# Cross-attention over 8 sequences: chunks of turned probabilities handed over singly, and one transpose moved ahead

## The chip, the cores and the metric

The kernel runs on one core of one Trainium2 chip. The metric is the time of one launch in microseconds (us) on the device. PE is TensorE, DVE is VectorE, ACT is ScalarE, POOL is GpSimd, and SP is SyncE, whose queue issues nearly all the DMAs.

## The reference

For each of 8 sequences of 1024 rows and 640 features, with 20 heads of 32 features, and an encoder context of 64 tokens, of which the last 8 are image tokens and 56 are text:

```python
q = split_heads(x @ w_q)
out_text = softmax(q @ k_text.T / sqrt(32)) @ v_text
out_ip   = softmax(q @ k_ip.T / sqrt(32) + box_mask) @ v_ip
out = (merge(out_text) + merge(out_ip)) @ w_out + b_out + x
```

`k_text`, `v_text`, `k_ip` and `v_ip` are projections of the context, and the mask depends on whether a row's grid position lies in one of four boxes.

## The kernel before

A setup (about the first 106 us) projects keys and values. After it the work goes in 16 groups `g` (`NG` is 16), each of 512 rows (`GQ`), two groups for each sequence (`GPB` is 2). A group has five chunks `m` of four heads each and ten pairs `p` of heads; chunk `m` holds pairs `2m` and `2m + 1`. Every product of the projections is made of three float32r products of high and low parts, `hi*hi + hi*lo + lo*hi`, so the tiles `xT`, `pT`, `oT` each have a `_hi` part, rounded by ACT, and a `_lo` part, the difference, made by DVE or POOL.

The groups are pipelined. While PE does the value products of group `g` (`pv_pair`, L1207 and L1208), it also makes the scores of group `n = g + 1` (L199), the output projection of groups `g - 1` and `g` (`out_step`) and the query projection of group `x = g + 2` (`q_steps`); the last two are matmuls of L101 to L103. Each engine runs an order written out by hand; a group has five slots on each engine, numbered nought to four, and slot `s` of PE begins with `pv_pair(g, 2s)` and `pv_pair(g, 2s + 1)`, followed by the scores of chunk `s` of `n`.

A chunk of probabilities passes these steps:

1. ACT copies the scores out of PSUM (`copy_scores`, L206); POOL adds the mask (`add_mask`, L242); DVE takes the maxima (`maxima`, L219); POOL subtracts them (`sub_max`, L248); ACT exponentiates (L211).
2. DVE sums and takes the reciprocal (`sums`, L225 and L227); POOL multiplies by it (`normalise`, L255) and raises `prob_done`.
3. DVE transposes 32x32 blocks into one of three stage buffers (`turn`, L236). `turn` waits for `prob_done` of its own chunk, and for the write to DRAM of the chunk three before it.
4. SP writes the stage to DRAM (`write_out`, L469) and, once that write has landed, reads it back rearranged in four DMAs (`read_back`, L474).
5. ACT makes `pT_hi` (L746) of each pair when the chunk has landed; DVE (even pairs, L981) or POOL (odd pairs, L599) makes `pT_lo`; PE multiplies.

The output of a pair goes by `move_pv` on ACT (L751) and `add_pv` on DVE (L991), then `oT_hi` on ACT (L755) and `oT_lo` on POOL (L595). `output` on DVE (L997) finishes a block of the result in `res`, SP stores it (L516) and reloads `res` (L490) once the store has landed.

In slot two of group `g` DVE has, in order, `add_pv(g, 4)`, `add_pv(g, 5)`, `pT_part(g, 6)`, `sums(n, 1)`, `maxima(n, 2)`, `turn(n, 0)`, `turn(n, 1)`, with `output(g - 1, 4)` after these in group 14 only, and then slot three begins: `add_pv(g, 6)`, `add_pv(g, 7)`, `pT_part(g, 8)`, `maxima(n, 3)`, `sums(n, 2)`. POOL's order there is `sub_max(n, 1)`, `normalise(n, 0)`, `add_mask(n, 2)`, `oT_part(g, 2)`, `normalise(n, 1)`, `sub_max(n, 2)`, `add_mask(n, 3)`, `pT_part(g, 9)`, `oT_part(g, 3)`, `sub_max(n, 3)`, `normalise(n, 2)`, `add_mask(n, 4)`, `normalise(n, 3)`, `pT_part(n, 1)`, `oT_part(g, 4)`. In slot four DVE has `add_pv(g, 8)`, `add_pv(g, 9)`, then for odd `g` the low parts of the next sequence's values (L425), then `sums(n, 3)`, `turn(n, 2)`, `maxima(n, 4)`, `pT_part(n, 0)`, `pT_part(n, 2)`, `turn(n, 3)`.

Group 14 is the last that prepares another one, and it has no queries of a next group to project. Its SP order has `store(13, 4)` and `load_res(14, 4)` between chunks 1 and 2 of group 15, and `store(13, 3)` with `load_res(14, 3)` ahead of chunk 0.

Of the kernel before, what the change touches and what calls it, by code (L numbers as in the profile page):

```python
# [29 lines left out]
def attention_kernel(nc, xT_dram, textT, ipT, bbox, w_q, w_k, w_v, w_k_ip, w_v_ip, w_out, b_out, grid_x, grid_y, outT):  # L30
# [30 lines left out]
    with whole:  # L61
# [54 lines left out]
        def x_lo_part(dve, g, k):  # L116
            dve.wait_ge(xT_hi_done, KD * g + k + 1)
            nc.vector.tensor_tensor(x_tile(xT_lo, k), x_of(g)[:, k, :], x_tile(xT_hi, k).bitcast(F32), ALU.subtract).then_inc(xT_lo_done, 1)
# [35 lines left out]
        def load_k(sp, b):  # L154
            sp.dma_start(k_raw[:].rearrange("p m k -> p (m k)"), k_scratch[:, b, :]).then_inc(k_raw_loaded, 16)
# [23 lines left out]
        def in_dram(eng, n):  # L179
            wait(eng, written[n % S_RING], 16 * (n // S_RING + 1))  # L180
# [3 lines left out]
        def chunk(m):  # L184
            return prob[:, m * CHUNK:(m + 1) * CHUNK].rearrange("p (r k) -> p r k", k=KEYS)
# [36 lines left out]
        def sums(dve, g, m):  # L222
            dve.wait_ge(exp_done, KD * g + m + 1)
            for n, (k0, k1) in enumerate(SPANS):
                nc.vector.tensor_reduce(total[:, m, n, :], chunk(m)[:, :, k0:k1], AX.X, ALU.add).then_inc(sum_done, 1)  # L225
            dve.wait_ge(sum_done, 2 * (KD * g + m + 1))
            nc.vector.reciprocal(inv[:, m, :, :], total[:, m, :, :]).then_inc(inv_done, 1)  # L227

        def turn(dve, g, m):

            n = KD * g + m
            dve.wait_ge(prob_done, n + 1)
            in_dram(dve, n - S_RING)
            src = prob[:, m * CHUNK:(m + 1) * CHUNK].rearrange("p (t h c i) -> p t h c i", t=GT, h=2, i=QUAD)
            dst = stage[:, n % S_RING].rearrange("p c h (t i) -> p t h c i", i=QUAD)
            nc.vector.transpose(dst, src).then_inc(turned, 1)  # L236
# [190 lines left out]
        with nc.Block() as block:  # L427

            @block.sync
            def _(sp):  # L430
# [34 lines left out]
                def write_out(g, m):  # L465
                    n = KD * g + m
                    sp.wait_ge(turned, n + 1)
                    wait(sp, pT_landed[m], 16 * QUADS * g)
                    sp.dma_start(p_scratch[m], stage[:, n % S_RING].rearrange("p c h t -> p (c h t)")).then_inc(written[n % S_RING], 16)  # L469

                def read_back(g, m):
                    in_dram(sp, KD * g + m)
                    for c in range(QUADS):
                        sp.dma_start(prob[c * QUAD:(c + 1) * QUAD, m * CHUNK:(m + 1) * CHUNK].rearrange("i (q f) -> i q f", q=QUADS),  # L474
                                     p_scratch[m].rearrange("(q i) (c f) -> c i q f", q=QUADS, c=QUADS)[c]).then_inc(pT_landed[m], 16)

                def hand_over(g, ms):
                    for m in ms:
                        write_out(g, m)
                    for m in ms:  # L480
                        read_back(g, m)

                def load_x(g):
                    sp.wait_ge(xT_lo_done, KD * (g - 1))
                    for k in range(KD):
                        sp.dma_start(x_of(g)[:, k, :], x_half[g % 2, g // 2][:, k, :]).then_inc(x_loaded[g % 2], 16)

                def load_res(g, m):
                    wait(sp, stored[m], 16 * g)
                    sp.dma_start(res[:, m, :], x_half[g % 2, g // 2][:, m, :]).then_inc(res_loaded[m], 16)  # L490
# [17 lines left out]
                def load_v(b):  # L508
                    sp.wait_ge(v_built, 2 * b)
                    for h in range(2):  # L510
                        sp.dma_start(v_raw[h * KEYS:h * KEYS + NTEXT, :], v_scratch.rearrange("(b k) d -> b k d", b=B)[b]).then_inc(v_raw_loaded, 16)
                        sp.dma_start(v_raw[h * KEYS + NTEXT:(h + 1) * KEYS, :], v_ip_scratch.rearrange("(b k) d -> b k d", b=B)[b]).then_inc(v_raw_loaded, 16)

                def store(g, m):
                    sp.wait_ge(out_done, outs_before(g, m) + 1)
                    sp.dma_start(out_half[g % 2, g // 2, m], res[:, m, :]).then_inc(stored[m], 16)  # L516
# [8 lines left out]
                for g in range(NG):  # L525
                    b = g // GPB
                    if g + 3 < NG:
                        load_x(g + 3)
                    if g > 0:
                        for m in range(3) if g == NG - 2 else OUT_ORDER:  # L530
                            store(g - 1, m)
                    hand_over(g, (4,))
                    for m in range(3) if g == NG - 2 else OUT_ORDER:
                        load_res(g, m)
                    if g == NG - 2:
                        store(g - 1, 3)
                        load_res(g, 3)
                    if g % GPB == 0 and b < B - 1:
                        sp.wait_ge(k_built, HPT * (b + 1))
                        load_k(sp, b + 1)  # L540
                        load_v(b + 1)
                    if g + 1 < NG:
                        hand_over(g + 1, (0, 1))
                        if g == NG - 2:
                            store(g - 1, 4)
                            load_res(g, 4)
                        hand_over(g + 1, (2, 3))
                for m in OUT_ORDER:
                    store(NG - 1, m)
                for m in range(KD):  # L550
# [316 lines left out]
            def _(dve):  # L867
# [138 lines left out]
                for g in range(NG):  # L1006
                    n, x = g + 1, g + 2
                    more, more_x = n < NG, x < NG

                    if more_x and g > 0:  # L1010
                        x_lo_part(dve, x, 0)
                    add_pv(g, 0)
                    add_pv(g, 1)
                    if g == 0:
                        maxima(dve, n, 0)
                        x_lo_part(dve, x, 0)
                    if more_x:
                        x_lo_part(dve, x, 1)
                        x_lo_part(dve, x, 2)
                    if 0 < g != NG - 2:  # L1020
                        output(g - 1, 3)
                    if more_x:
                        x_lo_part(dve, x, 3)
                    if g > 0:
                        sums(dve, g, 4)
                        if g != NG - 2:
                            output(g - 1, 4)
                        output(g - 1, 0)
                    if more and g > 0:
                        maxima(dve, n, 0)  # L1030
                    if g > 0:
                        output(g - 1, 1)
                        output(g - 1, 2)
                    if more_x:
                        x_lo_part(dve, x, 4)

                    add_pv(g, 2)
                    pT_part(g, 4)
                    add_pv(g, 3)
                    turn(dve, g, 4)  # L1040
                    if more:
                        maxima(dve, n, 1)
                        sums(dve, n, 0)
                    if g == NG - 2:
                        output(g - 1, 3)

                    add_pv(g, 4)
                    add_pv(g, 5)
                    pT_part(g, 6)
                    if more:  # L1050
                        sums(dve, n, 1)
                        maxima(dve, n, 2)
                        turn(dve, n, 0)
                        turn(dve, n, 1)
                    if g == NG - 2:
                        output(g - 1, 4)

                    add_pv(g, 6)
                    add_pv(g, 7)
                    pT_part(g, 8)  # L1060
                    if more:
                        maxima(dve, n, 3)
                        sums(dve, n, 2)

                    add_pv(g, 8)
                    add_pv(g, 9)
                    if more and n % GPB == 0:
                        v_lo_part(dve, n // GPB)
                    if more:
                        sums(dve, n, 3)  # L1070
                        turn(dve, n, 2)
                        maxima(dve, n, 4)
                        pT_part(n, 0)
                        pT_part(n, 2)
                        turn(dve, n, 3)
# [243 lines left out]
```

## Time and profile before

| | |
|---|---|
| time, median of 3 runs | 815.95 us (814.95 to 816.05) |
| the profiled execution | 814.83 us, span 813.0 us |
| granted TensorE clock, mean | 0.989 of full speed |
| PE busy | 794.7 us (98%) |
| DVE busy | 677.0 us (83%) |
| POOL busy | 629.1 us (77%) |
| ACT busy | 540.7 us (67%) |
| time of packets on SP's queue | 64.7% of 16 DMA engines |

Times inside the trace run from the start of the span. A row's start and duration are of one instruction or of several alike that follow each other ("x2"), and the bracket gives the idle time of the engine ahead of it and what ended that. A `tensor_reduce` or `normalise` of a chunk is two instructions, for the text keys and for the image keys, so one `sums` or one `sub_max` is a row of "x2". The group in which something happens can be told by PE: group 0 begins at 106.6, group 14 at 736.5 and group 15 at 774.65 us.

### The profile page before, as it was taken

The page shows a single profiled execution, that of the slowest core. Times are in us where ns is not written, and L with a number is a line of the kernel's source. Part 1 is how long each engine was busy: PE and PEld are TensorE (multiplying, and loading weights), DVE is VectorE, ACT ScalarE, POOL GpSimd, SP SyncE. Part 2 cuts the span into 40 slices and gives each one's busy share as a digit, 9 for nine tenths or more (in the row PEclk, how much of TensorE's full clock was granted, in tenths as well). Part 3 has the DMA queues.
Part 4 walks back from the last instruction along what each step waited for, and adds up shares of the span by engine and source line. Part 5 has one row for each costly group of instructions (what it writes and reads, how often), then busy time and mean ns, then how long its engine had stood idle before and what let it go on. Part 6 is the DMA issues. An engine that isn't in the chain of part 4 may idle for free.

```text
span 813.0 us, 12922 instructions
## 1 busy us (share of the span) xinstructions
PE 794.7 (98%) x4381; PEld 648.5 (80%) x4381; DVE 677.0 (83%) x983; ACT 540.7 (67%) x928; POOL 629.1 (77%) x576
## 2 busy tenths in 40 slices
PE   9999989999999999999999999999999999999887
PEld 8889867888788878888788888878887888787666
DVE  6938779889878897889878898889878888889973
ACT  7767367677586667666685767666775767676642
POOL 0049749797987888797979888797979888789972
PEclk9999989999999999999999999999999999999899
DMA  9943596765766577765766477665766476565664
GB/s 315 384 136 114 160 287 217 206 232 145 243 209 221 186 233 220 233 206 138 261 193 217 164 234 244 207 220 156 270 186 221 148 245 210 169 195 168 208 202 160
DMA packets 104177, 169.99 MB, mean 209 GB/s; under 512 B 13104, under 2 KB 56112, under 8 KB 103984
## 3 DMA queue, kind: packets, MB, share of 16 engines
q1 hardware_dynamic: 103968, 167.86, 64.7%
q10 hardware_dynamic: 144, 1.31, 0.4%
q8 instruction: 35, 0.57, 0.3%
q14 instruction: 30, 0.25, 0.1%
HBM read 103.26 MB, written 65.54 MB: 208 GB/s over the span
## 4 chain that ended last, share of the span: by engine, by line
PE 85%; POOL 6%; ACT 3%; DVE 2%; issue 1%; DMA 1%; SPq 1%; DVEq 0%; ACTq 0%
PE bank L101 22%; PE bank L102 21%; PE bank L103 21%; PE bank L199 9%; PE bank L1207 4%; PE bank L1208 4%; POOL prob L248 2%; POOL prob L255 1%; PE bank L1094 1%; PE bank L1102 1%; POOL wo_lo L558 1%; PE bank L1106 1%; POOL pT_lo L599 1%; ACT prob L206 1%; DVE stage L236 1%
## 5 line engine op out<-in xcount | busy, mean ns | idle before, releaser
L751 ACT ACTIVATE pv_part<-bank 64x512 f32<-64x512 f32 x160 | 94.7, 592 | 168.2 <-PE bank L1208 165.9
L248 POOL TENSOR_TENSOR prob<-prob,top 128x896 f32<-128x896 f32 (+1 forms) x160 | 183.0, 1164 | 13.3 <-DVE top L219 13.1
L255 POOL TENSOR_TENSOR prob<-prob,inv 128x896 f32<-128x896 f32 (+1 forms) x160 | 172.7, 1101 | 9.6 <-DVE inv L227 8.4
L991 DVE TENSOR_TENSOR o_raw<-bank,pv_part 64x512 f32<-64x512 f32 x160 | 110.1, 688 | 59.2 <-ACT pv_part L751 55.8
L101 PE MATMUL bank<-oT_hi,wo_hi 128*128 128x512 f32 x375 | 154.0, 411 | 2.4 <-POOL oT_lo L595 2.4
L101 PE MATMUL bank<-xT_hi,wq_hi 128*128 128x512 f32 x400 | 156.2, 390 | 0.0
L102 PE MATMUL bank<-xT_lo,wq_hi 128*128 128x512 f32 x400 | 155.9, 390 | 0.0
L103 PE MATMUL bank<-xT_hi,wq_lo 128*128 128x512 f32 x400 | 155.9, 390 | 0.0
L599 POOL TENSOR_TENSOR pT_lo<-prob,pT_hi 128x512 fp32r<-128x512 f32 x80 | 116.0, 1451 | 41.9 <-ACT pT_hi L746 41.8
L103 PE MATMUL bank<-oT_hi,wo_lo 128*128 128x512 f32 x375 | 146.7, 391 | 0.0
L102 PE MATMUL bank<-oT_lo,wo_hi 128*128 128x512 f32 x375 | 146.6, 391 | 0.0
L595 POOL TENSOR_TENSOR oT_lo<-o_raw,oT_hi 128x512 fp32r<-128x512 f32 x75 | 103.5, 1381 | 49.4 <-ACT oT_hi L755 47.9
L225 DVE TENSOR_REDUCE total<-prob 128x16 f32<-128x896 f32 (+1 forms) x160 | 101.8, 678 | 3.6 <-ACT prob L211 3.4
L219 DVE TENSOR_REDUCE top<-prob 128x16 f32<-128x896 f32 (+1 forms) x160 | 99.7, 664 | 4.0 <-ACT prob L206 2.6
L199 PEld LDWEIGHTS bank<-k_diag,qT 64*128 64x128 f32 x1280 | 79.1, 191 | 27.6 <-issue 22.4
L236 DVE STREAM_TRANSPOSE stage<-prob 128x1024 f32<-128x1024 f32 x80 | 96.7, 1223 | 0.9
L746 ACT ACTIVATE pT_hi<-prob 128x512 fp32r<-128x512 f32 x160 | 93.4, 624 | 4.4 <-DMA prob<-p_scratch 3.5
L199 PE MATMUL bank<-k_diag,qT 64*128 64x128 f32 x1280 | 94.1, 288 | 0.0
L206 ACT ACTIVATE prob<-bank 128x512 f32<-128x512 f32 x160 | 85.6, 592 | 12.2 <-PE bank L199 12.2
L211 ACT ACTIVATE prob<-prob 128x1024 f32<-128x1024 f32 x80 | 84.5, 1056 | 8.2 <-POOL prob L248 7.5
L101 PEld LDWEIGHTS bank<-oT_hi,wo_hi 128*128 128x128 f32 x375 | 70.3, 187 | 24.3 <-POOL oT_lo L595 3.5
L101 PEld LDWEIGHTS bank<-xT_hi,wq_hi 128*128 128x128 f32 x400 | 75.3, 188 | 15.8 <-issue 0.2
(111 smaller groups left out, 1276.1 us busy)
## 6 DMA issues: line engine op xcount, KB each, us to landing
p_scratch<-stage SPq DMA_DIRECT2D x80, 512.0 KB, 3.0
prob<-p_scratch SPq DMA_DIRECT2D x320, 128.0 KB, 3.1
res<-in_xT SPq DMA_DIRECT2D x80, 256.0 KB, 4.9
outT<-res SPq DMA_DIRECT2D x80, 256.0 KB, 3.9
xin<-in_xT SPq DMA_DIRECT2D x75, 256.0 KB, 4.7
w_raw<-in_L_xattn_w_k SPq DMA_DIRECT2D x8, 320.0 KB, 5.4
w_raw<-in_L_xattn_w_k_ip SPq DMA_DIRECT2D x8, 320.0 KB, 5.7
w_raw<-in_L_xattn_w_v_ip SPq DMA_DIRECT2D x8, 320.0 KB, 4.7
```

What stands on the lines that cost most here:

```text
L101: nc.tensor.matmul(dst, a_hi, b_hi, start=first, stop=False)
L102: nc.tensor.matmul(dst, a_hi, b_lo, start=False, stop=False)
L103: return nc.tensor.matmul(dst, a_lo, b_hi, start=False, stop=last)
L199: ins = nc.tensor.matmul(s_bank(g, 2 * m + r)[:, t * PW:(t + 1) * PW], qT[rows, m, q_cols], k_diag[rows, m, :], start=True, stop=True)
L219: ins = nc.vector.tensor_reduce(top[:, m, n, :], chunk(m)[:, :, k0:k1], AX.X, ALU.max)
L225: nc.vector.tensor_reduce(total[:, m, n, :], chunk(m)[:, :, k0:k1], AX.X, ALU.add).then_inc(sum_done, 1)
L236: nc.vector.transpose(dst, src).then_inc(turned, 1)
L248: ins = nc.gpsimd.tensor_tensor(s, s, top[:, m, n, :].unsqueeze(2).broadcast_to([P, ROWS, k1 - k0]), ALU.subtract)
L255: ins = nc.gpsimd.tensor_tensor(s, s, inv[:, m, n, :].unsqueeze(2).broadcast_to([P, ROWS, k1 - k0]), ALU.mult)
L595: nc.gpsimd.tensor_tensor(oT_at(oT_lo, g, m), o_raw[:, (KD * g + m) % 2, :], oT_at(oT_hi, g, m).bitcast(F32), ALU.subtract).then_inc(oT_lo ...
L599: nc.gpsimd.tensor_tensor(pT_part_at(pT_lo, g, p), pT(p), pT_part_at(pT_hi, g, p).bitcast(F32), ALU.subtract).then_inc(pT_lo_pool, 1)
L991: nc.vector.tensor_tensor(by_quadrant(raw), a, c, ALU.add).then_inc(pv_added, 1)
```

## The change

SP handles the chunks 0 to 3 of the next group one by one: it writes a chunk, waits for it to land, and issues its four reads, before it turns to the next chunk. Before, it wrote two and then read two. The first two hand-overs of group 0, ahead of the loop, stay couples. On DVE `turn(n, 0)` goes ahead of `sums(n, 1)` and `maxima(n, 2)`; `turn(n, 1)` stays where it was.

```diff
                     if g + 1 < NG:
-                        hand_over(g + 1, (0, 1))
+                        hand_over(g + 1, (0,))
+                        hand_over(g + 1, (1,))
                         if g == NG - 2:
                             store(g - 1, 4)
                             load_res(g, 4)
-                        hand_over(g + 1, (2, 3))
+                        hand_over(g + 1, (2,))
+                        hand_over(g + 1, (3,))
...
                     if more:
+                        turn(dve, n, 0)
                         sums(dve, n, 1)
                         maxima(dve, n, 2)
-                        turn(dve, n, 0)
                         turn(dve, n, 1)
```

## Rows read from the trace of the kernel before

**Rows 1.** Busy time by stretch: span, PE, PEld, DVE, ACT, POOL, clock, DMA share, GB/s
```profile
305.30:350.40 45.10, 45.10 (x254) 36.34 (x252) 37.53 (x56) 31.52 (x55) 37.78 (x36) 1.00 0.69 216
```

**Rows 2.** Timeline of PE: its waits in group 0 and in group 14
```profile
125.31 0.50 PE L101 MATMUL bank<-oT_hi,wo_hi 128*128 128x512 f32 x1 [0.64 <-POOL oT_lo L595]
...
764.64 0.77 PE L1207 MATMUL bank<-pT_hi,v_parts 128*128 128x512 f32 x1 [2.68 <-DVE pT_lo L981]
...
774.65 0.76 PE L1207 MATMUL bank<-pT_hi,v_parts 128*128 128x512 f32 x1 [2.66 <-DVE pT_lo L981]
```

**Rows 3.** Timeline of DVE, group 14, slots two and three
```profile
755.66 1.27 DVE L225 TENSOR_REDUCE total<-prob 128x16 f32<-128x896 f32 x2
756.96 0.35 DVE L227 RECIPROCAL inv<-total 128x32 f32<-128x32 f32 x1
...
758.36 2.60 DVE L236 STREAM_TRANSPOSE stage<-prob 128x1024 f32<-128x1024 f32 x2
...
763.09 1.41 DVE L981 TENSOR_TENSOR pT_lo<-prob,pT_hi 128x512 fp32r<-128x512 f32 x1
```

**Rows 4.** Timeline of POOL, group 14, slots two and three
```profile
753.50 2.50 POOL L255 TENSOR_TENSOR prob<-prob,inv 128x896 f32<-128x896 f32 x2
...
757.62 2.05 POOL L255 TENSOR_TENSOR prob<-prob,inv 128x896 f32<-128x896 f32 x2
759.64 2.06 POOL L248 TENSOR_TENSOR prob<-prob,top 128x896 f32<-128x896 f32 x2
...
762.68 1.27 POOL L599 TENSOR_TENSOR pT_lo<-prob,pT_hi 128x512 fp32r<-128x512 f32 x1 [0.56 <-ACT pT_hi L746]
```

**Rows 5.** Timeline of DVE, group 0, slots two and three
```profile
132.10 2.60 DVE L236 STREAM_TRANSPOSE stage<-prob 128x1024 f32<-128x1024 f32 x2
...
136.17 1.71 DVE L981 TENSOR_TENSOR pT_lo<-prob,pT_hi 128x512 fp32r<-128x512 f32 x1
```

**Rows 6.** Timeline of POOL, group 0, slots two and three
```profile
127.23 2.51 POOL L255 TENSOR_TENSOR prob<-prob,inv 128x896 f32<-128x896 f32 x2
...
136.03 1.30 POOL L599 TENSOR_TENSOR pT_lo<-prob,pT_hi 128x512 fp32r<-128x512 f32 x1 [0.17 <-ACT pT_hi L746]
```

**Rows 7.** Timeline of PE, group 0, the first matmul of slot four
```profile
138.55 0.39 PE L1207 MATMUL bank<-pT_hi,v_parts 128*128 128x512 f32 x1
```

**Rows 8.** Timeline of DVE, group 9, slots two, three and four
```profile
534.07 0.70 DVE L981 TENSOR_TENSOR pT_lo<-prob,pT_hi 128x512 fp32r<-128x512 f32 x1
...
541.73 0.69 DVE L981 TENSOR_TENSOR pT_lo<-prob,pT_hi 128x512 fp32r<-128x512 f32 x1
...
553.50 1.75 DVE L981 TENSOR_TENSOR pT_lo<-prob,pT_hi 128x512 fp32r<-128x512 f32 x1
```

**Rows 9.** Timeline of POOL, group 9, slot three
```profile
542.23 1.35 POOL L599 TENSOR_TENSOR pT_lo<-prob,pT_hi 128x512 fp32r<-128x512 f32 x1 [1.31 <-ACT pT_hi L746]
```

**Rows 10.** Timeline of PE, group 9 slot four and group 10 slot nought
```profile
544.75 0.39 PE L1207 MATMUL bank<-pT_hi,v_parts 128*128 128x512 f32 x1
...
555.82 0.39 PE L1207 MATMUL bank<-pT_hi,v_parts 128*128 128x512 f32 x1
```

**Rows 11.** Timeline of SP's queue, group 14: start and time of the issues
```profile
761.70 0.85 SPq L469 DMA_DIRECT2D p_scratch<-stage  x2
765.62 3.65 SPq L474 DMA_DIRECT2D prob<-p_scratch  x8
...
773.22 4.46 SPq L469 DMA_DIRECT2D p_scratch<-stage  x2
```

**Rows 12.** DMA issues of the page: size of each, median us to landing
```profile
p_scratch<-stage SPq DMA_DIRECT2D x80, 512.0 KB, 3.0
prob<-p_scratch SPq DMA_DIRECT2D x320, 128.0 KB, 3.1
```

**Rows 13.** Timeline of ACT: the waits for a landing in group 14, and group 15
```profile
744.01 1.15 ACT L746 ACTIVATE pT_hi<-prob 128x512 fp32r<-128x512 f32 x2 [2.15 <-DMA prob<-p_scratch]
...
788.85 1.15 ACT L746 ACTIVATE pT_hi<-prob 128x512 fp32r<-128x512 f32 x2
```

## The prediction

> **What bounds the kernel.** I read the busy times by stretch first. In a stretch of one period of the steady part, 45.1 us, PE is busy for all of it at the full granted clock (2.4 GHz), while DVE has 37.5 us of work and POOL 37.8 us [rows 1]. So PE alone sets the pace there; DVE, POOL and SP have cover, and nothing that the change does to them can make that part shorter. It can make it longer, where DVE or POOL come later than PE's next matmul needs them.
>
> Next I looked for PE's own waits. After the setup there are few. In group 0 there is one of 0.64 us [rows 2]. In group 14 there are two long ones, 2.68 us ahead of `pv_pair(14, 8)` and 2.66 us ahead of `pv_pair(15, 0)`, both ended by a `pT_lo` of DVE [rows 2]. Group 14 projects no queries, so PE has less work there than the two engines that feed it. The chain of waits runs there through POOL and then DVE, and touches just the slot that is edited: `turn(15, 1)` ends, then come `output(13, 4)`, two `add_pv` and `pT_part(14, 8)`, for which PE waits [rows 3].
>
> Last I read the order of DVE, POOL and SP around slot two, in group 14, in group 0, and in group 9 as one of the steady groups.
>
> **The change on DVE.** It adds no instruction; it moves a transpose of 1.25 us ahead of `sums(n, 1)` and `maxima(n, 2)`. Two things follow. `turn(n, 0)` must find `prob_done` of chunk 0 raised. And `sums(n, 1)` comes later, so `normalise(n, 1)` on POOL starts later, while between the sums and `turn(n, 1)` there is now one pair of maxima as cover in place of maxima and a transpose. Before, the second transpose found its chunk ready almost at once: two of them took 2.60 us for 2.50 us of work [rows 3].
>
> *Group 14.* `normalise(15, 0)` ends at 753.50 + 2.50 = 756.00 [rows 4]. DVE would have been free at 755.66 [rows 3], so it waits 0.4 us; the transpose runs from 756.04 and frees DVE at about 757.25. From the start of the sums to the end of the reciprocal it is 756.96 + 0.35 - 755.66 = 1.65 us [rows 3], so the reciprocal is there at 758.9. POOL, which before began `normalise(15, 1)` at 757.62 [rows 4], now begins at 758.95 and ends, with 2.05 us, at 761.0. DVE's maxima end at about 760.0, so DVE stands for 1 us, and `turn(15, 1)` ends at 762.3 in place of 760.96 [rows 3]: 1.35 us late. From there to the start of `pT_part(14, 8)` it was 763.09 - 760.96 = 2.13 us, so that now starts at 764.4. It took 1.41 us [rows 3] against 0.69 us in group 9 [rows 8], because POOL's `pT_part(14, 9)` was on its way; DVE ended 0.55 us after POOL's 762.68 + 1.27 = 763.95. POOL's own `pT_part(14, 9)` follows `sub_max(15, 2)` and a mask. That was 2.48 us from 759.64, less a wait of 0.56 us that falls away, but 0.46 us for the mask remains; it now starts at 761.0 + 2.06 + 0.4 = about 763.4 and ends at 764.65 [rows 4]. DVE then ends at 765.2 in place of 764.50, so the price is **0.7 us**. Its bounds are 0.6 us (if DVE gets in ahead of POOL, 764.4 + 0.7 = 765.1) and 1.35 us (the whole lateness). I take 0.7, since POOL's place shows which engine is ahead. What comes next moves with it: `maxima(15, 3)`, POOL's subtraction, the exponential, `sums(15, 3)`, `turn(15, 2)` and `pT_part(15, 0)` are the chain to the second wait of PE [rows 2], and from there to slot one of group 15 PE works without a wait. Nothing gives the 0.7 us back.
>
> *Group 0.* `normalise(1, 0)` ends at 127.23 + 2.51 = 129.74 [rows 6]. By the same steps: transpose to 130.95, reciprocal at 132.6, `normalise(1, 1)` to 134.75, `turn(1, 1)` to 136.05 in place of 132.10 + 2.60 = 134.70 [rows 5]. `pT_part(0, 8)` started 1.47 us after that end [rows 5] and now starts at 137.5. POOL, 1.3 us late as well, has `pT_part(0, 9)` from 137.15 to 138.45 (it took 1.30 us [rows 6]), so DVE ends 0.55 us behind that, at 139.0. PE starts 0.14 us after such an end (764.50 to 764.64 in group 14), at 139.15; it was due at 138.55 [rows 7]. The price is **0.6 us**, with nought as the lower bound: were DVE ahead of POOL, it would end at 138.2 and hide. A short wait like the one of 0.64 us costs itself: the first matmul after it took 0.50 us, those after long waits 0.77 us [rows 2].
>
> *The steady groups.* In group 9 `normalise` of chunk 0 is long done when DVE is through with `pT_part(9, 6)` at 534.77 [rows 8]. The transpose, the sums and the reciprocal end at 534.7 + 1.2 + 1.65 = 537.5; POOL ends `normalise(10, 1)` at 539.65, and `turn(10, 1)` ends at 540.9, 1.2 us later than before. Part of it goes into a wait of DVE for `pv_part` that was there. `pT_part(9, 8)` arrives at 542.4 in place of 541.73 [rows 8], and this time POOL's `pT_part(9, 9)`, which starts at 542.23 [rows 9], is ahead. With 1.29 us for POOL and 0.55 us behind it DVE ends at 544.1 in place of 542.4. PE needs it at 544.75 [rows 10], so with 0.14 us it is hidden with 0.5 us left. In odd groups DVE has the values' low parts in slot four, and there the rest of the lateness, 0.35 us, gets through to `pT_part(10, 0)`. That ended at 553.50 + 1.75 = 555.25 [rows 8] and will end at 555.6; PE needs it at 555.82 [rows 10]. With 0.14 us that is hidden by less than 0.1 us. I take **nothing** for the 14 groups between; from the other side it is 0.3 us in each of the 7 odd ones, 2.1 us.
>
> The Trainium skill (SBUF — State Buffer, "SBUF: two separate sides") calls the port pair that DVE and GpSimd share an exclusive lock: whichever starts first has it for the whole instruction. By it the three prices hang on who arrives first, and by its rule alone, with DVE first, the sum would be 0.6 us less, from group 0. The trace agrees with the lock: 1.41 and 1.71 us against 0.69 us for one and the same instruction.
>
> **The change on SP.** It adds no DMA, but each couple becomes two round trips. Couple 2 and 3: `turn(n, 3)` comes 5 us after `turn(n, 2)`, so write and reads of chunk 2 fit in between, chunk 2 lands about 3 us earlier, and chunk 3 as before. Couple 0 and 1: chunk 0 is read earlier, and the write of chunk 1 now stands behind the landing and the four reads of chunk 0, so chunk 1 lands later: about 3 us, a landing of 3.0 us [rows 12], where SP comes late. In the steady groups ACT asks for chunk 1 more than 10 us after its transpose: hidden. In group 14 SP gets to chunk 0 at 761.70 [rows 11], behind a reload of `res`, so the earlier transpose brings nothing there.
>
> Then it adds up. The reads of the couple ended at 765.62 + 3.65 = 769.27 [rows 11]. Now: chunk 0 read by 767.4, chunk 1 written then, landed 3.0 us on and read by 772.3. Store and reload took SP 773.22 - 769.27 = 3.95 us before the write of chunk 2 [rows 11], now at 776.2; landed 779.2, read by 781.1, chunk 3 written, landed 784.1, read by 785.9, and in place 3.1 us later [rows 12], at **789.0**. ACT takes chunk 3 at 788.85 + 0.6 + 0.6 [rows 13], that is at 790.1 with the 0.7 and 0.6 us of PE. It is hidden with 1 us left. If each landing takes 3.92 us, as 761.70 to 765.62 did [rows 11], chunk 3 comes at 791.8 and costs 1.7 us.
>
> The Trainium skill (DMA: Bandwidth & Descriptors, "Anatomy of one DMA") puts a DMA at about 2.0 us fixed plus its bytes at 436 GB/s. For 512 KB that is an estimate of 3.2 us, between the two of this trace; by it four landings add 0.8 us to 789.0 and the chunk is still in time. The rule speaks against the change all the same: a second fixed cost is paid for each couple.
>
> **The sum.** 0.7 + 0.6 = 1.3 us on the profiled execution's 814.83 us. That execution lies 1.1 us under the median of the runs, so against the median of 815.95 us it is **817.2 us**, 0.16% more. What a measurement of this kernel can tell from no change is 0.2%, 1.6 us, so this counts as the same.
>
> **The rivals.**
>
> *A. Late chunk 3 in group 15.* SP's four round trips in a row run past 790.1. For it: there is only 1 us left, and landings of 3.9 us occur [rows 11]. Against it: the median is 3.0 us [rows 12]. It gives 817.2 + 0 to 1.7, say 818.3 us.
>
> *B. The steady cover gives way.* PE waits for `pT_part(n, 0)` in the odd groups. For it: a margin under 0.1 us by my own steps. Against it: PE has no wait there now, and a later PE gives the others more time. 7 x 0.3 us give 817.2 + 2.1 = 819.3 us.
>
> *C. Nothing shows.* DVE arrives ahead of POOL in group 0, and some of group 14's lateness is absorbed: 0 to 0.6 us, 816.2 us.
>
> *D. Faster, by the earlier chunk 2 of group 14.* ACT stood for 2.15 us for its landing at 744.01 [rows 13]. With the reads of chunk 2 issued about 3 us earlier this wait goes. It decides only if `pT_part(14, 4)` or `(14, 5)` hold the chain there. Against it: in the chain of waits it is POOL that works there without a pause, and its row shows no wait for `pT_hi` before the one of 0.56 us [rows 4]. If all 2.15 us came through, the time would be 815.95 - 2.15 = 813.8 us.
>
> **Chances.** The forecast (0.7 and 0.6 us, each within its bounds) 0.47, A 0.15, B 0.15, C 0.14, D 0.09. The forecast's own range is 816.5 to 817.9 us, and some 0.1 of its 0.47 lies beyond 1.6 us. Slower: 0.15 + 0.15 + 0.1 = 0.40, less 0.01 of A that stays under. Faster: D. The rest, 0.52, is the same. The range of 8 in 10 takes in A, most of B and C: 815.6 to 819.6 us.
>
> **What would show it.** In the profile after: `turn(15, 0)` begins at 756.0 plus what was lost before, DVE idles about 1 us ahead of `turn(15, 1)`, released by POOL's L255; PE's wait ahead of `pv_pair(14, 8)` grows from 2.68 to about 3.4 us; in group 0 a wait of PE of 0.6 us appears ahead of L1207; none in groups 1 to 13; ACT's wait of 2.15 us at 744 is gone; SP has writes of x1 in place of x2. I am wrong if PE waits in the steady groups, if `pT_part(15, 6)` waits for a landing, or if the order of DVE and POOL at the shared work is the other one.

## The result, and the profile after

The changed kernel takes 819.88 us (median of 6 runs, 817.39 to 823.73), the kernel before 815.08 us (6 runs, 813.39 to 816.05). The ratio is 1.0066, with a 95% interval of 1.0041 to 1.0091: slower by about 5 us. (A ratio here is an estimate from all the runs of both kernels, and not the quotient of the two medians, which is 1.0059; what is said of single parts of the time comes from profiled executions.) I had 817.2 us with a range up to 819.6, and "the same" as the likeliest. So the size was missed, and the median lies outside the range. Both numbers are medians of runs; against 815.08 my sum of 1.3 us would have been 816.4.

The profiled execution took 817.39 us, span 815.6, which is the fastest of the six. Its span is 2.6 us longer than that of the kernel before; a second profiled execution of the same kernel, shown further down, took 819.05 us.

Of PE's waits in the changed kernel these four bear on the account, from its timeline. The first answers to a matmul that waited for nothing before [rows 7], the last two to [rows 2]:

```profile
138.44 0.47 PE L1209 MATMUL bank<-pT_hi,v_parts 128*128 128x512 f32 x1 [0.34 <-DVE pT_lo L983]
...
603.49 1.16 PE L199 MATMUL bank<-k_diag,qT 64*128 64x128 f32 x16 [1.16 <-ACT qT L142]
...
767.20 0.77 PE L1209 MATMUL bank<-pT_hi,v_parts 128*128 128x512 f32 x1 [3.36 <-DVE pT_lo L983]
...
777.20 0.77 PE L1209 MATMUL bank<-pT_hi,v_parts 128*128 128x512 f32 x1 [2.66 <-DVE pT_lo L983]
```

The first and the third are the two prices that I had put into the sum. In group 14 the wait is 3.36 - 2.68 = 0.68 us longer (forecast 0.7); counted from the scores of slot nought of that group, the matmul starts after 767.20 - 739.03 = 28.17 us in place of 764.64 - 737.35 = 27.29, so the group loses 0.88 us, and 0.2 us of it fall ahead of the place that I had looked at, 0.1 of them at a matmul that waits for `res` (0.44 in place of 0.33 us). In group 0 the row shows 0.34 us of idle time, but matmuls overlap in the trace, so the loss is read from starts: from the scores of slot three to those of slot four it took PE 131.27 to 139.52, 8.25 us, in place of 131.88 to 139.55, 7.67 us. That is 0.58 us (forecast 0.6). The second I had not: at the turn from group 10 to group 11 PE waits 1.16 us for the last query tile before it can make scores.

DVE in group 14, the answer to [rows 3]. The transpose of chunk 0 waits 0.30 us for `normalise(15, 0)`, that of chunk 1 waits 1.03 us for `normalise(15, 1)`:

```profile
757.92 1.25 DVE L236 STREAM_TRANSPOSE stage<-prob 128x1024 f32<-128x1024 f32 x1 [0.30 <-POOL prob L255]
759.09 1.24 DVE L225 TENSOR_REDUCE total<-prob 128x16 f32<-128x896 f32 x2
760.36 0.35 DVE L227 RECIPROCAL inv<-total 128x32 f32<-128x32 f32 x1
...
762.88 1.25 DVE L236 STREAM_TRANSPOSE stage<-prob 128x1024 f32<-128x1024 f32 x1 [1.03 <-POOL prob L255]
...
766.26 0.79 DVE L983 TENSOR_TENSOR pT_lo<-prob,pT_hi 128x512 fp32r<-128x512 f32 x1
```

DVE in group 9, the answer to [rows 8]. `pT_part(9, 8)` takes 1.72 us in place of 0.69, because POOL's `pT_part(9, 9)` now starts ahead of it (at 542.49, and 542.61 for DVE):

```profile
542.61 1.72 DVE L983 TENSOR_TENSOR pT_lo<-prob,pT_hi 128x512 fp32r<-128x512 f32 x1
```

What is new is in SP's queue. Group 10 in the changed kernel, start and time of each issue (L469 writes a chunk, L474 reads it back, L490 reloads `res`):

```profile
578.20 2.56 SPq L490 DMA_DIRECT2D res<-in_xT  x5
...
582.84 0.34 SPq L469 DMA_DIRECT2D p_scratch<-stage  x1
589.70 1.74 SPq L474 DMA_DIRECT2D prob<-p_scratch  x4
591.54 0.38 SPq L469 DMA_DIRECT2D p_scratch<-stage  x1
597.38 1.73 SPq L474 DMA_DIRECT2D prob<-p_scratch  x4
```

The reads of a chunk are issued when its write has landed. So the write of chunk 0 took 6.86 us and that of chunk 1 another 5.84 us. The first is no exception: in groups 0 to 13 the write of chunk 0 takes 5.3 to 7.0 us. The second is: the write of chunk 1 takes 3.2 to 4.2 us in the others, and over 5 only in groups 10 and 11; no run shows what held it there. The last read of chunk 1 is issued at 599.1. And ACT, whose timeline at that place is

```profile
601.32 0.63 ACT L748 ACTIVATE pT_hi<-prob 128x512 fp32r<-128x512 f32 x1 [2.88 <-DMA prob<-p_scratch]
601.85 0.58 ACT L142 ACTIVATE qT<-bank 128x512 f32<-128x512 f32 x1
602.33 0.62 ACT L748 ACTIVATE pT_hi<-prob 128x512 fp32r<-128x512 f32 x1
602.85 0.59 ACT L142 ACTIVATE qT<-bank 128x512 f32<-128x512 f32 x1
```

stands 2.88 us for chunk 1, in `pT_part(11, 2)`. Behind it in ACT's order are `move_q(12, 3)`, `pT_part(11, 3)` and, as the first of group 11, `move_q(12, 4)` at 602.85. PE's scores of group 12 need that one; they start at 603.49. The product that chunk 1 is for comes a slot later and was not held up.

In group 9, an odd one, the same part of SP's queue before, and then after:

```profile
538.66 1.46 SPq L469 DMA_DIRECT2D p_scratch<-stage  x2
542.39 3.64 SPq L474 DMA_DIRECT2D prob<-p_scratch  x8
```

```profile
533.72 2.33 SPq L490 DMA_DIRECT2D res<-in_xT  x5
536.20 0.33 SPq L469 DMA_DIRECT2D p_scratch<-stage  x1
542.76 1.75 SPq L474 DMA_DIRECT2D prob<-p_scratch  x4
```

The totals by waiting engine say the same. Waits of ACT for the landing of a chunk were 3.5 us in 3 places before; after, in sum, times and longest:

```profile
ACT pT_hi L748 <- DMA prob<-p_scratch: 17.8, 12, 3.1
...
SPq L474 <- DMA p_scratch<-stage: 274.2, 78, 6.6
```

The chain of waits ends, in place of PE and POOL work, with SP's four round trips for the chunks of group 15. This is its part from the write of chunk 2 to POOL's `pT_part(15, 7)`; the columns are start, duration, and what the chain goes through:

```profile
778.07 4.08 DMA p_scratch<-stage
...
784.01 3.27 DMA p_scratch<-stage
...
788.59 2.78 DMA prob<-p_scratch
791.37 0.02 issue
791.39 0.02 ACT pT_hi L748
...
792.62 1.30 POOL pT_lo L601
```

Chunk 3 lands at 791.37, and ACT takes it at 791.39. That the chain runs there does not mean that it costs much: PE's wait behind it, ahead of `out_step(15, m, 1)`, is 1.37 us, and was 1.35 us before.

### The profile page after: what moved, and what is told of

Same layout as the page of the kernel before. It is cut to its first block, busy times and chain, and to the rows that moved or that the text cites. A ratio compares the mean times of both kernels' runs of the same rounds, so it can differ in the third digit from the quotient of the medians.

```text
span 815.6 us, 12922 instructions
## 1 busy us (share of the span) xinstructions
PE 795.1 (97%) x4381; PEld 647.5 (79%) x4381; DVE 689.7 (85%) x983; ACT 542.0 (66%) x928; POOL 634.4 (78%) x576
## 4 chain that ended last, share of the span: by engine, by line
PE 79%; POOL 8%; DVE 4%; DMA 3%; ACT 3%; SPq 2%; issue 1%; DVEq 0%; ACTq 0%
PE bank L101 21%; PE bank L102 19%; PE bank L103 19%; PE bank L199 9%; PE bank L1209 4%; PE bank L1210 4%; POOL prob L248 3%; POOL prob L255 2%; DMA p_scratch<-stage 2%; SPq L474 1%; PE bank L1096 1%; DVE stage L236 1%; PE bank L1104 1%; POOL pT_lo L601 1%; POOL wo_lo L560 1%
## 5 line engine op out<-in xcount | busy, mean ns | idle before, releaser
L597 POOL TENSOR_TENSOR oT_lo<-o_raw,oT_hi 128x512 fp32r<-128x512 f32 x75 | 107.3, 1430 | 47.5 <-ACT oT_hi L757 47.5
L748 ACT ACTIVATE pT_hi<-prob 128x512 fp32r<-128x512 f32 x160 | 94.6, 625 | 18.8 <-DMA prob<-p_scratch 17.8
L983 DVE TENSOR_TENSOR pT_lo<-prob,pT_hi 128x512 fp32r<-128x512 f32 x80 | 92.6, 1165 | 12.5 <-ACT pT_hi L748 11.2
```

The source lines that it names most:

```text
L597: nc.gpsimd.tensor_tensor(oT_at(oT_lo, g, m), o_raw[:, (KD * g + m) % 2, :], oT_at(oT_hi, g, m).bitcast(F32), ALU.subtract).then_inc(oT_lo ...
```

## The experiments

All ratios are to the kernel before, run on the same chip in the same job.

**The two parts apart.** First the moved transpose alone, with couples on SP (the edit is against the changed kernel):

```diff
-                        hand_over(g + 1, (0,))
-                        hand_over(g + 1, (1,))
+                        hand_over(g + 1, (0, 1))
...
-                        hand_over(g + 1, (2,))
-                        hand_over(g + 1, (3,))
+                        hand_over(g + 1, (2, 3))
```

> The moved transpose alone; SP hands over in couples as before. Theory 1 (the loss is chunk 1 that lands late by SP's serial round trips, and ACT stands for it with the queries behind): here chunk 1 is written with chunk 0 and lands in time, so only the two places at the ends remain, 0.34 us in group 0 and 0.68 us ahead of pv_pair(14, 8): ratio 1.001 to 1.002, no wait of PE in groups 1 to 13. Theory 2 (the loss is DVE and POOL, 1.2 us later in each slot two): nearly the whole loss is here, ratio 1.005 or more, with PE waits for pT_lo or oT_lo in the steady groups.

Measured: 816.04 us, ratio 1.0020 (1.0012 to 1.0029). Its waits of PE are those of the sum, the one of 0.34 us in group 0 and

```profile
765.89 0.77 PE L1207 MATMUL bank<-pT_hi,v_parts 128*128 128x512 f32 x1 [3.44 <-DVE pT_lo L981]
```

and none for `qT`. Theory 2 falls. This part alone costs about what I had forecast for the whole. By its profile it is 0.6 us in group 0, 0.5 us in the steady groups (the table further down) and 0.9 us from the scores of group 14 to the end.

Then SP's single hand-over alone, with DVE's order as before (against the changed kernel):

```diff
-                        turn(dve, n, 0)
                         sums(dve, n, 1)
                         maxima(dve, n, 2)
+                        turn(dve, n, 0)
                         turn(dve, n, 1)
```

> SP hands over singly, DVE's order as before. Theory 1: most of the loss is here, ratio 1.003 to 1.006; ACT waits for landings 8 times or more, some over 2.5 us, and where they are over 2.5 us PE waits for qT ahead of the scores of the next slot nought. Theory 2: ratio 0.999 to 1.001.

Measured: 818.37 us (12 runs, 815.52 to 821.23), ratio 1.0045 (1.0030 to 1.0060). ACT waits for landings in 11 places, up to 4.15 us, and PE for `qT` in two; one of them, and the place in group 15 where chunk 3 is late, from the timelines of PE and ACT:

```profile
332.07 1.16 PE L199 MATMUL bank<-k_diag,qT 64*128 64x128 f32 x16 [0.48 <-ACT qT L142]
...
796.16 0.50 PE L101 MATMUL bank<-oT_hi,wo_hi 128*128 128x512 f32 x1 [1.74 <-POOL oT_lo L597]
...
792.36 1.16 ACT L748 ACTIVATE pT_hi<-prob 128x512 fp32r<-128x512 f32 x2 [0.41 <-DMA prob<-p_scratch]
```

That last wait of PE was 1.35 us in the kernel before. The two parts together give 1.0020 x 1.0045 = 1.0065, beside 1.0066 for the change. The intervals are 0.2 to 0.5% wide, so that the two agree so closely is luck.

**Which couple.** Only chunks 2 and 3 singly:

```diff
                         hand_over(g + 1, (0, 1))
...
-                        hand_over(g + 1, (2, 3))
+                        hand_over(g + 1, (2,))
+                        hand_over(g + 1, (3,))
```

> Only chunks 2 and 3 singly, chunks 0 and 1 as a couple, DVE's order as before. Theory 1: chunk 1 lands in time, chunk 2 sooner: ratio 0.998 to 1.001, no wait of PE in the steady groups, ACT's wait of 2.15 us at 744 moves to chunk 3. Theory 2: the same. If it is over 1.003, the loss comes from chunks 2 and 3 and both fall.

Measured: 814.53 us, ratio 0.9997 (0.9989 to 1.0006). The transposes of these two begin about 5 us apart on DVE (551.23 and 556.87 in group 9 before), so splitting them alone costs nothing and gains nothing. The loss needs chunks 0 and 1 split.

**What stands behind the late chunk.** The changed kernel, with ACT's order so that no query move follows the landing:

```diff
                         pT_part(n, 0)
                         pT_part(n, 1)
-                        pT_part(n, 2)
                     if more_x:
                         move_q(act, x, 3)
-                    if more:
-                        pT_part(n, 3)
...
                         if more:
                             move_q(act, n, 4)
+                        pT_part(g, 2)
+                        pT_part(g, 3)
```

and DVE with `turn(n, 3)` ahead of `pT_part(n, 2)`.

> The changed kernel, but ACT makes pT_hi(n, 2) and (n, 3) behind both of the query moves that follow them (move_q(x, 3) and the next group's move_q(n, 4)), and DVE turns chunk 3 ahead of pT_part(n, 2). Chunk 1 lands as late as in the changed kernel, but nothing of the queries stands behind it. Theory 1: the steady loss goes, PE has no wait for qT, ratio 1.001 to 1.003 (what is left is that of the transpose alone). Theory 2: the loss stays, 1.005 or more.

Measured: 817.86 us (817.73 to 818.99), ratio 1.0042 (1.0029 to 1.0054). It lies between the two theories' numbers. PE has no wait for `qT`, and ACT's waits for landings fall from 17.8 us in 12 places to

```profile
ACT pT_hi L748 <- DMA prob<-p_scratch: 3.9, 3, 2.6
```

with the steady ones gone. The write of chunk 0 is as slow as in the changed kernel (5.5 to 6.9 us in groups 0 to 13), so the wait of PE for `qT` comes by way of ACT's order: that is the mechanism of theory 1. By time alone this run does not show it, for its interval overlaps that of the change. What is left is more than the transpose, and the profile says where: the steady part is 1.25 us longer than before, 0.51 of which are the transpose's, with steps of up to 0.23 us at the end of odd groups, and from the scores of group 14 on it is 0.5 us longer than with the transpose alone. Chunk 3 does not arrive late here. So this order has a price of its own, about 1.2 us.

**Where the single hand-over costs.** Chunks 0 and 1 singly in groups 0 to 13 only, then all four singly in group 14 only, both with DVE's order as before:

```diff
-                        hand_over(g + 1, (0, 1))
+                        for ms in ((0,), (1,)) if g < NG - 2 else ((0, 1),):
+                            hand_over(g + 1, ms)
```

```diff
-                        hand_over(g + 1, (0, 1))
+                        for ms in ((0, 1),) if g < NG - 2 else ((0,), (1,)):
+                            hand_over(g + 1, ms)
...
-                        hand_over(g + 1, (2, 3))
+                        for ms in ((2, 3),) if g < NG - 2 else ((2,), (3,)):
+                            hand_over(g + 1, ms)
```

> Chunks 0 and 1 singly in groups 0 to 13 alone, a couple in group 14; chunks 2 and 3 a couple everywhere; DVE's order as before. Theory A (the loss of the single hand-over sits in the steady groups: chunk 1 late, ACT, queries): ratio 1.002 to 1.004, waits of PE for qT in the profile of some. Theory B (it sits in group 15, where four round trips of SP in a row end at chunk 3): ratio 0.999 to 1.001.

> All four chunks singly in group 14 alone, couples elsewhere; DVE's order as before. Theory A: ratio 0.999 to 1.001. Theory B: 1.002 to 1.004, and ACT waits for the landing of chunk 3 at about 790 with a wait of PE ahead of out_step(15, m, 1) longer than 1.35 us. Both can hold in part: then this ratio and that of the steady one multiply to 1.0045, the ratio of all hand-overs single.

Measured: 816.57 us, ratio 1.0025 (1.0016 to 1.0035), and 816.12 us, ratio 1.0015 (1.0005 to 1.0026). Both theories hold in part; 1.0025 x 1.0015 = 1.0040, beside 1.0045 for all. The profiled execution of the first was its fastest run (815.26 us), and it shows no wait of PE for `qT` and no loss in the steady part; ACT waited for landings in 14 places, the longest 2.2 us. So its 1.0025 is not seen in its own profile, and that it is the wait for `qT` is taken from the profiles of the other kernels. In the second, ACT waits for chunk 3, and PE behind it 1.92 us in place of 1.35:

```profile
789.28 1.15 ACT L748 ACTIVATE pT_hi<-prob 128x512 fp32r<-128x512 f32 x2 [0.60 <-DMA prob<-p_scratch]
...
793.06 0.50 PE L101 MATMUL bank<-oT_hi,wo_hi 128*128 128x512 f32 x1 [1.92 <-POOL oT_lo L597]
```

That wait accounts for 0.57 us. From the scores of group 14 to the end this execution took 77.38 us, the kernel before 75.65. Most of the other 1.2 us comes of TensorE's clock: behind a wait of 5.49 us ahead of `pv_pair(15, 0)` it was 0.86 up to this wait, against 0.92 before. The eased kernel further down, which has couples there, has the like, 0.85. So of the 1.0015 the late chunk is shown for about half.

**Why the write of chunk 0 is slow.** The changed kernel, with the reloads of `res` behind the hand-over of chunk 1:

```diff
-                    for m in range(3) if g == NG - 2 else OUT_ORDER:
+                    for m in range(3) if g == NG - 2 else () if 0 < g < NG - 2 else OUT_ORDER:
                         load_res(g, m)
...
                         hand_over(g + 1, (1,))
+                        for m in OUT_ORDER if 0 < g < NG - 2 else ():
+                            load_res(g, m)
```

> The changed kernel with the five reloads of res in groups 1 to 13 issued behind the hand-over of chunk 1 in place of ahead of chunk 0, so that the write of chunk 0 does not share the queue with them. If these loads are what keeps the write of chunk 0 at 6 to 7 us, it lands in 3 to 4 us, chunk 1 about 3 us sooner, and ACT's waits in the steady groups go; ratio 1.002 to 1.005 in place of 1.0066. If the write is slow for another reason: ratio as changed, 1.006 to 1.007.

Measured: 817.17 us, ratio 1.0032 (1.0021 to 1.0043). SP in group 9:

```profile
535.53 0.34 SPq L469 DMA_DIRECT2D p_scratch<-stage  x1
538.17 1.73 SPq L474 DMA_DIRECT2D prob<-p_scratch  x4
540.49 0.34 SPq L469 DMA_DIRECT2D p_scratch<-stage  x1
543.27 1.73 SPq L474 DMA_DIRECT2D prob<-p_scratch  x4
545.05 2.33 SPq L490 DMA_DIRECT2D res<-in_xT  x5
```

The write of chunk 0 lands in 2.64 us; in the changed kernel the same one, issued at 536.20, took 6.56 us. In all of groups 1 to 13 it now takes 2.6 to 3.7 us, also in the even ones, where the loads of keys and values still stand ahead of it; in group 0, where the reloads stay in front, it takes 5.97. The waits for landings are gone from groups 1 to 13, and what is left is near the transpose (1.0020) times the end (1.0015). So the loads of 1.25 MB just ahead of it are what holds the write.

**All of it eased.** The single hand-over with both causes removed: `res` late in groups 1 to 13, couples in group 14, DVE's order as before.

```diff
-                    for m in range(3) if g == NG - 2 else OUT_ORDER:
+                    for m in range(3) if g == NG - 2 else () if 0 < g < NG - 2 else OUT_ORDER:
                         load_res(g, m)
...
-                        hand_over(g + 1, (0, 1))
+                        for ms in ((0,), (1,)) if g < NG - 2 else ((0, 1),):
+                            hand_over(g + 1, ms)
+                        for m in OUT_ORDER if 0 < g < NG - 2 else ():
+                            load_res(g, m)
...
-                        hand_over(g + 1, (2, 3))
+                        for ms in ((2,), (3,)) if g < NG - 2 else ((2, 3),):
+                            hand_over(g + 1, ms)
```

> All chunks singly in groups 0 to 13, in groups 1 to 13 with the reloads of res behind chunk 1; couples in group 14; DVE's order as before. If the loss of the single hand-over is made of nothing but the late chunk 1 in the steady groups and the four round trips at the end: ratio 0.999 to 1.001. If a single hand-over has another cost: 1.002 or more.

Measured: 815.70 us against 815.24, ratio 1.0006 (0.9997 to 1.0014). The single hand-over has no third cost that this can tell from nothing. The delay has gone with the loads: in group 9 the write of chunk 0 lands in 2.64 us, and that of chunk 2, now behind them, takes 6.57 us, where no engine but SP waits for it:

```profile
548.18 2.33 SPq L490 DMA_DIRECT2D res<-in_xT  x5
551.22 0.33 SPq L469 DMA_DIRECT2D p_scratch<-stage  x1
557.79 1.75 SPq L474 DMA_DIRECT2D prob<-p_scratch  x4
```

**A second profile of the changed kernel.**

> The changed kernel once more, for a second profile. If its spread (817.4 to 823.7 us) comes from how late chunks land, other groups than group 10 have the wait of PE for qT, and ACT's waits for landings are other ones; the wait of 0.34 us in group 0 and that of 3.4 us ahead of pv_pair(14, 8) are the same.

Measured: 819.05 us. The waits of 0.34 us in group 0 and 3.33 us in group 14 are there again. PE's wait for `qT`, in sum, times and longest, and one of its places:

```profile
PE bank L199 <- ACT qT L142: 2.7, 4, 0.9
...
331.55 1.16 PE L199 MATMUL bank<-k_diag,qT 64*128 64x128 f32 x16 [0.66 <-ACT qT L142]
```

It has four of them, each at the end of an even group, at other groups than the first profile, which had its only one at the turn to group 11 (the end of group 10). The table takes from the timelines of PE the time between the scores of slot nought of group 1 and of group 14:

| kernel | from | to | us |
|---|---|---|---|
| before | 150.62 | 737.35 | 586.73 |
| changed, profile of the 817.39 us | 150.59 | 739.03 | 588.44 |
| changed, profile of the 819.05 us | 149.77 | 740.39 | 590.62 |
| transpose alone | 150.37 | 737.61 | 587.24 |
| single hand-over alone | 150.99 | 739.51 | 588.52 |
| chunks 0 and 1 singly, groups 0 to 13 | 150.94 | 737.70 | 586.76 |
| changed, ACT's order eased | 150.83 | 738.81 | 587.98 |
| changed, `res` late | 149.91 | 737.15 | 587.24 |
| eased | 149.39 | 736.12 | 586.73 |

Beyond the 0.51 us of the transpose the changed kernel loses 1.20 us there in one profile and 3.38 us in the other, of which its waits for `qT` are 1.16 and 2.7 us.

**A version that beats both.** The profile says that DVE's order binds the end of group 14. Two moves there, in group 14 alone, first with chunks 2 and 3 singly, then with all couples:

```diff
-                    if g == NG - 2:
-                        output(g - 1, 4)
...
+                    if g == NG - 2:
+                        output(g - 1, 4)
                     if more:
                         sums(dve, n, 3)
+                        if g == NG - 2:
+                            pT_part(n, 0)
                         turn(dve, n, 2)
                         maxima(dve, n, 4)
-                        pT_part(n, 0)
+                        if g < NG - 2:
+                            pT_part(n, 0)
```

> Chunks 2 and 3 singly with couple 0 and 1, and in group 14 alone DVE makes pT_part(15, 0) ahead of turn(15, 2) and maxima(15, 4), and output(13, 4) only behind add_pv(14, 9). If the end of group 14 is bound by DVE's order, as the two waits of PE say, pv_pair(14, 8) starts some 1.4 us sooner and pv_pair(15, 0) 2 to 3 us sooner, and the end by 1.2 to 1.6 us (pv_pair(15, 1) waits for POOL): ratio 0.998. If POOL alone binds it: 0.9995 to 1.

> The kernel before with the two moves of DVE in group 14 alone (pT_part(15, 0) ahead of turn(15, 2) and maxima(15, 4); output(13, 4) behind add_pv(14, 9)), all hand-overs in couples. If the gain of the run before belongs to DVE's order alone: ratio 0.998 to 0.999. If it needed the single hand-over of chunks 2 and 3: 0.9995 to 1.

Measured: 813.80 us, ratio 0.9986 (0.9977 to 0.9994), and 814.26 us against 815.24, ratio 0.9989 (0.9980 to 0.9998). Both are faster than before, by about 1 us, and the gain is that of DVE's order. PE in the second:

```profile
763.00 0.47 PE L1210 MATMUL bank<-pT_hi,v_parts 128*128 128x512 f32 x1 [1.36 <-DVE pT_lo L981]
...
772.50 0.76 PE L1210 MATMUL bank<-pT_hi,v_parts 128*128 128x512 f32 x1 [4.28 <-DVE pT_lo L981]
774.01 0.77 PE L1210 MATMUL bank<-pT_hi,v_parts 128*128 128x512 f32 x1 [0.31 <-POOL pT_lo L599]
```

From the start of group 14's scores, `pv_pair(15, 0)` begins after 772.50 - 737.06 = 35.4 us in place of 774.65 - 737.35 = 37.3. That is 1.9 us sooner, where 2 to 3 were expected; `pv_pair(14, 8)`, at 763.00, is 1.35 us sooner, as expected.

## Why the prediction was right or wrong

*PE sets the pace of the steady part, and nothing there can be gained.* Right: 586.73 to 586.76 us in the seven kernels that keep DVE's order there and show no wait for `qT`, the kernel before among them.

*Group 14, 0.7 us.* Right, by its steps, for the wait: 0.68 us, with waits of DVE of 0.30 and 1.03 us where I had 0.4 and 1. `pT_part(14, 8)` took only 0.79 us, since it began at 766.26, shortly before POOL's `pT_part(14, 9)` ended at 766.50, and it ended 0.55 us behind that end, as worked out. The group as a whole lost 0.88 us, the 0.2 us ahead of it not being in the sum. (One step is worded wrongly: from the start of `sub_max(15, 2)` to that of `pT_part(14, 9)` it was 3.04 us, which without the wait of 0.56 is the prediction's 2.48 us; its result is not touched.)

*Group 0, 0.6 us.* Right: 0.58 us, with POOL's `pT_part(0, 9)` ahead of DVE's `pT_part(0, 8)`, which ended 0.54 us behind it.

*The steady groups on DVE, nothing.* Nearly. In the transpose alone the steady part is 0.51 us longer, in steps of about 0.07 us at the end of each of the 7 odd groups, where `pT_part(n, 0)` is due. The margin under 0.1 us that I had worked out was in truth just under nought. Rival B was this mechanism, at a quarter of the price that I gave it.

*Chunk 2 sooner.* It came: ACT no longer waits for chunk 2 at 744. But a wait for chunk 3 stands in its place, and nothing is gained:

```profile
747.32 0.64 ACT L748 ACTIVATE pT_hi<-prob 128x512 fp32r<-128x512 f32 x1 [2.05 <-DMA prob<-p_scratch]
```

Rival D falls.

*Chunk 1 later, hidden.* **This is the step that failed:** "In the steady groups ACT asks for chunk 1 more than 10 us after its transpose: hidden." In group 10 it asked at 598.4 for a chunk whose transpose ended at 586.3, and it had it at 601.3, 15 us after the transpose. I had taken one landing of 3.0 us [rows 12] as the price of the second round trip. It is a median over all writes, most of which are not issued behind 1.25 MB of loads. The write of chunk 0 is. In group 9 it was issued at 538.7 before and landed at 542.4; now it is issued 2.5 us sooner, at 536.2, and lands at 542.8. So the head start was worth nothing, and the write of chunk 1, which had been next to it in the queue, now starts after that. I had also not named what is queued behind `pT_part(n, 2)` on ACT, which is the queries that PE needs for its scores. The runs put 1.0025 on this, and the profiles of the changed kernel 1.2 and 3.4 us.

*The end, chunk 3 with 1 us left.* The margin was used up: the four landings took 3.76, 3.58, 4.09 and 3.28 us, where the sum had 3.92 for the first and 3.0 for each of the others. But in both profiled executions of the changed kernel PE's wait behind chunk 3 is longer by no more than 0.02 us. The chunk was late, by 0.41 and 0.60 us, in two kernels without the moved transpose, the single hand-over alone and that in group 14 alone. Rival A is thus a near miss where it was meant, and the 1.0015 of the runs is that of the kernel with DVE's order as before.

So the sum had 1.0016 in it for the transpose, which measured 1.0020, and nothing for SP's serial round trips, which measured 1.0045. Multiplied from the runs of the parts, 1.0020 x 1.0025 x 1.0015 = 1.0060 lies inside the interval of the change (1.0041 to 1.0091). The Trainium skill (DMA: Bandwidth & Descriptors, "Anatomy of one DMA") gives, for DMAs issued from GpSimd, about 2.0 us fixed plus the bytes at 436 GB/s, which for 512 KB is an estimate of 3.2 us. By it the writes would have been on time. These writes are issued from SP, so it is the figure of another path than theirs, which the prediction did not say; the trace has 2.64 us for a write without the loads ahead, somewhat less, and 6.56 us behind them. (Four landings at that estimate do not add 0.8 us to the prediction's 789.0, whose first landing is one of 3.92 us: the other three add 0.6.)

What stays open: in unprofiled runs I can't see which group lost the time. The spread, highest less lowest, does not settle it. It is 6.3 us in the changed kernel, 5.7 with the single hand-over alone, 4.7 with `res` late and 4.4 with all four singly in group 14, but 2.5 us with chunks 0 and 1 singly in groups 0 to 13, and 2.0 to 3.1 us in the others that do not split all four chunks in group 14. So it goes with the four round trips in group 14 and not with the steady ones (only the kernel with ACT's order eased, 1.3 us from 5 runs, does not fit), and why it does is not shown.

## What to carry to other kernels

A couple of write-then-read transfers on one queue shares its wait; splitting it makes the second pay a whole round trip, unless the two come further apart than that anyway, as chunks 2 and 3 did. Price that round trip by the write at this very place, with what is issued just ahead of it, and not by the median of all writes. Then ask what is queued behind the engine that takes the data: here a product that was due a slot later held up, through the order of ACT, a query tile that was due at once.

## What the runs showed of the hardware

Two landings of one and the same 512 KB write differ by 2.5 times, by what was issued just ahead of it: 2.64 us, and 6.56 us behind five loads of 256 KB. Over 13 groups it is 2.6 to 3.7 us against 5.3 to 7.0.

TensorE's clock after a wait differs between executions that wait alike, and the bill comes later. After its wait of 2.7 us in group 14, the granted clock in the next 7.3 us was 0.57 in the kernel before, so most of it at the lower of its two levels, 1.2 GHz, and 1.00 in the eased kernel, which is 2.4 GHz. The columns are the stretch, its length, busy time of PE, PEld, DVE, ACT and POOL, the granted clock, DMA share and GB/s; first the kernel before, then the eased one:

```profile
764.64:771.90 7.26, 7.25 (x29) 5.30 (x29) 6.89 (x12) 4.76 (x8) 6.73 (x7) 0.57 0.84 255
774.65:782.20 7.55, 7.55 (x27) 6.15 (x28) 5.52 (x6) 2.77 (x4) 6.00 (x5) 0.80 0.69 226
```

```profile
764.30:771.60 7.30, 4.50 (x29) 3.21 (x29) 6.92 (x12) 5.05 (x9) 6.78 (x7) 1.00 0.83 225
774.30:781.90 7.60, 7.59 (x21) 6.11 (x22) 4.20 (x5) 2.76 (x4) 5.98 (x5) 0.61 0.60 206
```

With the full clock PE was done sooner, waited 5.51 us in place of 2.66 for the same `pT_lo`, and then had the low clock for longer, in a stretch where it sets the pace. From there to the matmul that waits for `oT_lo(15, 1)` it took 793.66 - 774.30 = 19.4 us in place of 792.64 - 774.65 = 18.0. That is 1.4 us, as much as the effects studied here, and a reason not to read one profiled execution for less than that. It is not a matter of the kernel alone: in the two profiled executions of the changed kernel the clock in the 7.3 us after waits of 3.36 and 3.33 us was 0.58 and 0.77, and the next wait was 2.66 and 3.99 us.
